# Attention a from a transposed copy of x with its norm behind the projection, the last norm's scale behind its linear layer, and a new order

## The chip, the cores and the metric

The kernel runs on one core of a Trainium2 chip. The metric is the time of one execution on the device in microseconds. Its engines are TensorE (PE, matrix products), VectorE (DVE), ScalarE (ACT), GpSimd (POOL) and SyncE (SP, which issues the DMAs). SBUF is the working memory, PSUM holds what TensorE writes: eight banks of 128 x 512 fp32.

## What is computed

Four blocks in a row on `x` of 4 batches x 256 rows x 512 columns, each behind a LayerNorm and with a residual:

```
x = x + attn_a(layernorm(x), Wqkv, bqkv, Wo, bo)     # one head, d = 128, softmax over 256 keys
x = x + ffn(layernorm(x), qweight, scale, zero, bias)
x = x + attn_b(layernorm(x), wq, wk, wv, wo)         # 32 heads of 16, rotary, causal
x = x + ffn(layernorm(x), qweight, scale, zero, bias)
return x

def layernorm(x):  return (x - mean(x)) / sqrt(var(x) + 1e-5)
def attn_a(x):     qkv = x @ Wqkv + bqkv;  q, k, v = split(qkv, 3)
                   return (softmax(q @ k.T / sqrt(128)) @ v) @ Wo + bo
def ffn(x):        weight = (unpack4(qweight) - zero) * scale     # [512 out, 512 in]
                   return x @ weight.T + bias
```

## The kernel before, in words

The work is cut into steps: a name, a batch `b` or a unit `u`, and a tile `t` of 128 rows (two tiles a batch). One list, PLAN, holds all 1004 steps. Each engine walks through the list and takes its own steps in that order, so the order in the list is the order on every engine; between engines there are semaphores, one for each kind of step. SP has its loads (D), stores and the copies between DRAM and SBUF in the same list, and issues them in order.

The steps around the change, in the kernel before:

- D loads: `x` by tile of 128 x 512, `wqkv` in two parts (columns of v, and of q and k), `bqkv`, `bias_o`, `q` (the packed weights), `ww` (the four weights of attention b, 1 MB each), and others.
- LN (DVE, L740 and L741) takes mean and variance. RS (GpSimd, L531 to L535) makes `rstd` and `offset` = -mean x rstd in four small instructions. NO (ScalarE, L602) writes the normed tile XN = x * rstd + offset. T (PE, L883) transposes it in four pieces, TH (ScalarE, L580) copies the transposed tile to `XT_hi` in the rounded type fp32r, and TL (DVE, L745) writes the rest, `XT_lo`. This chain stands in front of all four blocks; s = 1 to 4 in a step's name is the block.
- A product of two such pairs is three matmuls (`three_pass`, L859 to L861): low x high, high x low, high x high. QH, VH, QL and VL split Wqkv in the same way.
- Attention a of a batch: QV and QK project (q, k and v come out transposed), VC and QC copy them out with the bias, VA and AC transpose v back, SA is q k', AM the row maximum, AE the exponential, ET and EC its transpose, OA the product with v, OC its copy, WA the product with Wo (L931), WD (DVE, L768) divides by the sum and adds to X. BA (GpSimd, L541) adds the bias to X.
- ffn: F (PE, L941 and L942) is two matmuls for each piece of 128 inputs, FS (DVE, L774) adds the share of `zero`, FD (DVE, L782 and L784) multiplies by `scale` and adds to X. In the last block of batch 3 F and FD go by halves of 256 columns.
- Attention b: PJ, RO, RP, P1 to P3 project and rotate q and k; S, MX, ST, EX, MK, PV are the scores, the maxima, the exponentials, the mask and the product with v; NA, NX, NB, DH, DL carry the result to WO (PE), and OD (DVE, L788) adds it to X. OS stores.
- KP (PE, L869) are matmuls on `ident_h` whose results nobody reads.

Of the kernel before, what the change touches and what calls it, by code (L numbers as in the profile page):

```python
# [1062 lines left out]
```

## Time and profile before

| | |
|---|---|
| median of 3 runs | 273.88 us (273.66 to 274.55) |
| the profiled execution | 273.11 us, span of its trace 271.4 us |
| PE busy | 257.7 us, 95% |
| DVE busy | 225.8 us, 83% |
| GpSimd busy | 185.3 us, 68% |
| ScalarE busy | 145.2 us, 54% |
| DMA | 31.86 MB, mean 117 GB/s |

An engine's busy time is the union of its instructions' spans. The spans of matmuls overlap, since the next one enters while the one before drains; what one costs in a full stream is the distance from start to start. The span begins at 0 us with the first instruction; the execution's own time is 1.7 us longer. The clock that was granted to TensorE is shown as full in all 40 slices of the page.

### The profile page before, as it was taken

The numbers are of one execution on the slowest core, as the hardware profiler recorded it, in microseconds if no ns is written. First come the engines' busy times: TensorE is split into PE (matmuls) and PEld (weight loads), VectorE is DVE, ScalarE is ACT, GpSimd is POOL, SyncE is SP. The second block draws the span as 40 slices with busy tenths as digits, with TensorE's granted clock in tenths as the row PEclk, the third lists the DMA queues.
The fourth block names the chain that finished last, engine by engine and source line by source line (L and its number), as shares of the span: only waits on it lengthen the run. The fifth ranks groups of instructions, "written<-read, shape, count | busy, mean of one in ns | idle before, by whom it ended". The sixth has DMA issues, their size and how long they took to land.

```text
span 271.4 us, 6548 instructions
## 1 busy us (share of the span) xinstructions
PE 257.7 (95%) x2368; PEld 212.5 (78%) x2368; DVE 225.8 (83%) x402; ACT 145.2 (54%) x239; POOL 185.3 (68%) x229
## 2 busy tenths in 40 slices
PE   7698999999999999999999999999998999999984
PEld 2597878798989988778887988889677877785753
DVE  4575669668999998989868998998999988767886
ACT  2759796732774565365631767616634663277040
POOL 5887679989896889964568697287736663167070
PEclk9999999999999999999999999999999999999999
DMA  7999130202536237343343433343363333120112
GB/s 218 293 386 387 71 82 1 80 0 82 151 112 181 81 101 189 90 137 112 107 127 111 131 90 89 98 121 91 110 176 111 87 114 100 42 78 2 41 39 79
DMA packets 51192, 31.86 MB, mean 117 GB/s; under 512 B 5400, under 2 KB 46552, under 8 KB 51160
## 3 DMA queue, kind: packets, MB, share of 16 engines
q1 hardware_dynamic: 51160, 31.44, 38.5%
q8 instruction: 19, 0.31, 0.5%
q14 instruction: 13, 0.11, 0.1%
HBM read 22.91 MB, written 8.39 MB: 115 GB/s over the span
## 4 chain that ended last, share of the span: by engine, by line
PE 55%; POOL 13%; SPq 10%; DVE 6%; issue 6%; ACT 5%; DMA 3%; ACTq 0%; POOLq 0%; DVEq 0%
PE psum L859 10%; PE psum L860 9%; PE psum L861 9%; SPq L487 8%; PE psum L1026 7%; PE psum L1011 4%; PE psum L989 4%; POOL wb_lo L550 3%; POOL X L541 3%; POOL rstd L534 3%; PE psum L941 2%; PE psum L942 2%; PE psum L883 2%; PE psum L987 2%; PE psum L1013 2%
## 5 line engine op out<-in xcount | busy, mean ns | idle before, releaser
L573 POOL TENSOR_SCALAR_AFFINE_SELECT E<-E 128x512 f32<-128x512 f32 x64 | 41.5, 676 | 32.1 <-ACT E L699 32.0
L812 DVE TENSOR_REDUCE nmax<-psum 128x4 f32<-128x512 f32 (+1 forms) x64 | 59.2, 943 | 3.5 <-PE psum L989 3.5
L699 ACT ACTIVATE E<-psum 128x1536 f32<-128x1536 f32 x32 | 46.3, 1446 | 24.9 <-PE psum L1013 17.0
L859 PE MATMUL psum<-XT_lo,wb_hi 128*128 128x256 f32 x128 | 38.3, 299 | 0.3 <-POOL wb_lo L550 0.2
L860 PE MATMUL psum<-XT_hi,wb_lo 128*128 128x256 f32 x128 | 36.1, 282 | 0.0
L861 PE MATMUL psum<-XT_hi,wb_hi 128*128 128x256 f32 x128 | 36.1, 282 | 0.0
L602 ACT ACTIVATE XN<-X,offset,rstd 128x512 f32<-128x512 f32 x32 | 25.5, 810 | 19.2 <-POOL offset L535 19.2
L580 ACT ACTIVATE parts<-SH 128x512 bf16<-128x512 f32 x32 | 19.9, 626 | 25.4 <-POOL SH L562 17.2
L859 PE MATMUL psum<-wb_lo,XT_hi 128*128 128x256 f32 (+1 forms) x96 | 33.0, 344 | 0.0
L989 PE MATMUL psum<-QK 128*128 128x128 bf16 x256 | 30.2, 220 | 0.9 <-DMA QK<-qk_parts 0.6
L745 DVE TENSOR_TENSOR XT_lo<-psum,XT_hi 128x512 fp32r<-128x512 f32 x32 | 21.5, 682 | 11.0 <-ACT XT_hi L580 10.9
L860 PE MATMUL psum<-wb_hi,XT_lo 128*128 128x256 f32 (+1 forms) x96 | 30.6, 319 | 0.0
L861 PE MATMUL psum<-wb_hi,XT_hi 128*128 128x256 f32 (+1 forms) x96 | 30.5, 318 | 0.0
L1026 PE MATMUL psum<-E,V 128*32 128x128 f32 (+1 forms) x512 | 27.2, 331 | 1.6 <-POOL E L573 0.7
L941 PE MATMUL psum<-wf,XT_lo 128*128 128x512 f32 (+1 forms) x72 | 27.2, 387 | 0.1
L859 PEld LDWEIGHTS psum<-XT_lo,wb_hi 128*128 128x128 f32 x128 | 24.3, 190 | 2.6 <-DVE XT_lo L745 1.2
L942 PE MATMUL psum<-wf,XT_hi 128*128 128x512 f32 (+1 forms) x72 | 25.9, 369 | 0.0
L580 ACT ACTIVATE XT_hi<-psum 128x512 fp32r<-128x512 f32 x32 | 18.6, 598 | 13.1 <-PE psum L883 13.0
L740 DVE BATCH_NORM_STATS2 stats<-X 128x6 f32<-128x512 f32 x32 | 21.9, 684 | 4.4 <-DMA X<-L_attn_a_x 3.9
L1011 PE MATMUL psum<-QK 98*128 98x256 bf16 x128 | 24.8, 274 | 0.6 <-ACT E L699 0.4
L566 POOL TENSOR_TENSOR SH<-SH,parts 128x512 f32<-128x512 f32 x16 | 19.6, 1223 | 7.7 <-ACT parts L580 7.7
L860 PEld LDWEIGHTS psum<-XT_hi,wb_lo 128*128 128x128 f32 x128 | 24.4, 191 | 0.1
(97 smaller groups left out, 683.5 us busy)
## 6 DMA issues: line engine op xcount, KB each, us to landing
QK<-qk_parts SPq DMA_DIRECT2D x192, 64.0 KB
qk_parts<-parts SPq DMA_DIRECT2D x16, 384.0 KB, 2.9
X<-L_attn_a_x SPq DMA_DIRECT2D x8, 256.0 KB, 5.6
out<-X SPq DMA_DIRECT2D x6, 256.0 KB, 2.1
wb_raw<-L_attn_b_wq SPq DMA_DIRECT2D x1, 1024.0 KB, 9.7
wb_raw<-L_attn_b_wk SPq DMA_DIRECT2D x1, 1024.0 KB, 12.7
wb_raw<-L_attn_b_wv SPq DMA_DIRECT2D x1, 1024.0 KB, 15.0
wb_raw<-L_attn_b_wo SPq DMA_DIRECT2D x1, 1024.0 KB, 13.8
```

What stands on the lines that cost most here:

```text
L573: last = nc.gpsimd.affine_select(out=e, in_=e, compare_op=ALU.is_ge, fill=0.0, base=0, pattern=[[0, GH], [1, P]], channel_multiplier=-1)
L580: return nc.scalar.activation(out_, in_, ACT.Copy)
L699: nc.scalar.activation(E[:, n % 2], bank(3, 3), ACT.Exp, scale=float(HD) ** -0.5).then_inc(done[k], 1)
L812: nc.vector.tensor_reduce(nmax[:, u % 2, g::NG, t], (bank(1, 2) if t else bank(0)).rearrange("p (h k) -> p h k", h=GH), AX, ALU.max, negat ...
L859: nc.tensor.matmul(out_, stat[0], mov[1], start=first, stop=False)
L860: nc.tensor.matmul(out_, stat[1], mov[0], start=False, stop=False)
L861: return nc.tensor.matmul(out_, stat[0], mov[0], start=False, stop=last)
L941: nc.tensor.matmul(ps, XT_lo[:, slot, kt, tok], wf[:, kt, cols], start=kt == 0, stop=False)
L942: last = nc.tensor.matmul(ps, XT_hi[:, slot, kt, tok], wf[:, kt, cols], start=False, stop=kt == KT - 1)
L989: last = nc.tensor.matmul(ps[:, (j + 1) * width - P:(j + 1) * width], q[:, h, t * P:width], kk[:, h, t * P:width], start=True, stop=True)
L1011: nc.tensor.matmul(bank(3, 2)[:, j * S:(j + 1) * S], kk[0:SROWS, h, 0:P], q[0:SROWS, h, :], start=True, stop=True)
L1026: last = nc.tensor.matmul(ps[j * 32:(j + 1) * 32, kt * P:S], values(u // 2)[:, kt, (u % 2) * UH + NG * j + g], E[:, n % 2, at:at + S - kt ...
```

## The change

Attention a no longer needs the chain through T in front of it. The kernel gets a second input, `x_transposed`, x transposed by batch, 2 MB in all, made on the host beside the other inputs. XH (ScalarE) and XL (DVE) split it as it is, without the norm. QA projects x itself: the stationary side is a piece of `x_transposed`, the moving side 384 columns of Wqkv, so q, k and v come out by rows. The norm is applied afterwards: x_normed @ W = rstd * (x @ W) + offset * colsum(W). CS makes the column sums with a matrix of ones, CE copies them, Z (ScalarE) makes offset * colsum for a tile, QE (DVE) multiplies QA's sum by rstd and adds Z. QT transposes q and k; v is used as QE leaves it, so QV, QK, VC, VA and AC are gone. The bias of v goes through Wo once: BC spreads it, BM multiplies, BO adds it to `bias_o`. Wqkv is loaded and split in four pieces of 128 rows. Free buffers hold the raw pieces: XN, O and E for x, half of E for q, k and v, TR for the sums.

In the last block of batch 3 (SCALED_LATE), NO subtracts only the mean, and waits for LN instead of RS. RS makes `offset` = -rstd, RW multiplies the row sum by it, and FD multiplies the product by `offset` as well as `scale`.

PLAN is new as a whole, 1033 steps. KP at the start is 14 matmuls before and 8 now; at the end 2 x 5 before and 5 now.

```
-    ("D", "x", 0, 0), ("LN", 1, 0, 0), ("KP", 14), ("RS", 1, 0, 0), ("NO", 1, 0, 0), ("T", 1, 0, 0), ("D", "x", 0, 1),
+    ("D", "xt", 1, 0), ("D", "wqkv", 0), ("D", "xt", 0, 0), ("XH", 1, 0), ("XL", 1, 0), ("QH", 0), ("QL", 0), ("KP", 8),
...
+SCALED_LATE = (4, B - 1)
...
+        def tiles(b, i):
+            return slice(i, i + 1) if b == 0 else slice(2 * i, 2 * i + 2)
...
+        def raw(b, i):
+            if b < 2:
+                return XN[:, 2 * b:2 * b + 2].rearrange("p a (k n) -> p (a k) n", n=S)[:, tiles(b, i)]
+            if b == 2:
+                return O[:, tiles(b, i)]
+            return E[:, 0, 0:KT * S].rearrange("p (k n) -> p k n", n=S)[:, tiles(b, i)]
+
+        def qkv(b, t):
+            return E[:, 1, ((b % 2) * NT + t) * 3 * DA:((b % 2) * NT + t + 1) * 3 * DA]
...
+                    if (s, b) == SCALED_LATE:
+                        link(nc.gpsimd.tensor_scalar(mv[:, sl, ts, 1], mv[:, sl, ts, 1], EPS, None, ALU.add))
+                        link(nc.gpsimd.tensor_tensor(rstd[:, sl, ts], mv[:, sl, ts, 1], minus_half[:, ts], ALU.pow))
+                        nc.gpsimd.tensor_scalar(offset[:, sl, ts], rstd[:, sl, ts], -1.0, None, ALU.mult
+                                                ).then_inc(done[k], 1)
+                        continue
...
+                elif k == "XH":
+                    act.wait_ge(loaded["xt", *st[1:]], 16)
...
+                    copy(XT_hi[:, xt_of[st], tiles(*st[1:])], raw(*st[1:])).then_inc(done[k], 1)
...
+                    nc.scalar.activation(qkv(b, t), col_sum, ACT.Identity, scale=offset[:, b, t:t + 1]).then_inc(done[k], 1)
...
+                    if (s, b) == SCALED_LATE:
+                        act.wait_ge(done["LN"], upto("LN", s, b, t))
...
+                elif k == "XL":
...
+                    nc.vector.tensor_tensor(XT_lo[:, slot, part], raw(*st[1:]), XT_hi[:, slot, part].bitcast(F32),
+                                            ALU.subtract).then_inc(done[k], 1)
...
+                    nc.vector.scalar_tensor_tensor(qkv(b, t), bank(bank_of["QA", b, t, 0])[:, 0:3 * DA], rstd[:, b, t:t + 1],
+                                                   qkv(b, t), ALU.mult, ALU.add).then_inc(done[k], 1)
...
+                    for kt in range(KT):
+                        nc.tensor.matmul(ps, ones[:], wqkv_lo[:, kt], start=kt == 0, stop=False)
+                        last = nc.tensor.matmul(ps, ones[:], wqkv_hi[:, kt], start=False, stop=kt == KT - 1)
...
+                    for kt in range(KT)[tiles(b, i)]:
+                        last = three_pass(ps, [xt[:, slot, kt, t * P:(t + 1) * P] for xt in (XT_hi, XT_lo)],
+                                          [w[:, kt] for w in (wqkv_hi, wqkv_lo)], kt == 0, kt == KT - 1)
```

The loads at the start, as SP issues them. Before:

```order
L430 DMA X<-L_attn_a_x 128x512 x4
L432 DMA wqkv_raw<-L_attn_a_Wqkv 128x4x128
L432 DMA wqkv_raw<-L_attn_a_Wqkv 128x4x256
L437 DMA bias_o<-L_attn_a_bo 128x512
L430 DMA X<-L_attn_a_x 128x512 x2
L434 DMA bqkv_c<-L_attn_a_bqkv 128x3x1
```

Now (XN is the buffer that holds the raw pieces of `x_transposed` of batches 0 and 1, in pieces of 128 or 256 of the 512 inputs):

```order
L469 DMA XN<-x_transposed 128x512
L467 DMA wqkv_raw<-L_attn_a_Wqkv 128x384
L469 DMA XN<-x_transposed 128x256
L467 DMA wqkv_raw<-L_attn_a_Wqkv 128x384
L471 DMA bqkv_c<-L_attn_a_bqkv 128x3x1
L467 DMA wqkv_raw<-L_attn_a_Wqkv 128x384
L469 DMA XN<-x_transposed 128x256
L467 DMA wqkv_raw<-L_attn_a_Wqkv 128x384
L465 DMA X<-L_attn_a_x 128x512
```

The tiles of x themselves, which led the queue, now begin in ninth place; `bqkv` has moved from tenth to fifth.

The end on DVE, from the last low parts of attention b's output (`XT_lo<-O`) to the last blocks of batch 3. Before:

```order
L750 TENSOR_TENSOR XT_lo<-O,XT_hi 128x128
L745 TENSOR_TENSOR XT_lo<-psum,XT_hi 128x4x128
L750 TENSOR_TENSOR XT_lo<-O,XT_hi 128x128
L788 TENSOR_TENSOR X<-X,psum 128x512
L740 BN_STATS stats<-X 128x6
L741 BN_AGGR mv<-stats 128x2
L788 TENSOR_TENSOR X<-X,psum 128x512
L740 BN_STATS stats<-X 128x6
L741 BN_AGGR mv<-stats 128x2
L774 SCALAR_TENSOR_TENSOR X<-shift_r,row_sum,X 128x512
L782 TENSOR_TENSOR psum<-psum,scale_r 128x512
L784 TENSOR_TENSOR X<-X,psum 128x512
```

Now:

```order
L834 TENSOR_TENSOR XT_lo<-O,XT_hi 128x128 x2
L834 TENSOR_TENSOR XT_lo<-O,XT_hi 128x3x128
L829 TENSOR_TENSOR XT_lo<-psum,XT_hi 128x4x128
L879 TENSOR_TENSOR X<-X,psum 128x512
L824 BN_STATS stats<-X 128x6
L825 BN_AGGR mv<-stats 128x2
L860 SCALAR_TENSOR_TENSOR X<-shift_r,row_sum,X 128x512
L879 TENSOR_TENSOR X<-X,psum 128x512
L824 BN_STATS stats<-X 128x6
L825 BN_AGGR mv<-stats 128x2
L829 TENSOR_TENSOR XT_lo<-psum,XT_hi 128x4x128
```

OD (`X<-X,psum`) and LN of the second tile stood right behind those of the first; now FS of the batch before stands between them. On PE the four steps before the last ones were WO(3,1,0), WO(3,0,0), WO(3,1,1), WO(3,0,1); now they are WO(3,0,0), T(4,2,1), WO(3,0,1), WO(3,1,0), WO(3,1,1), and then T(4,3,0), F(4,2,1), F(4,3,0,0), five matmuls of KP, T(4,3,1) and the other three halves of F.

## Rows read from the trace of the kernel before

**Rows 1.** Head of the page: span, busy time and share by engine, instructions.
```profile
span 271.4 us, 6548 instructions
PE 257.7 (95%) x2368; PEld 212.5 (78%) x2368; DVE 225.8 (83%) x402; ACT 145.2 (54%) x239; POOL 185.3 (68%) x229
```

**Rows 2.** DVE by stretch: from:to, length, busy us (instructions), clock, DMA share, GB/s.
```profile
11.00:30.00 19.00, 12.74 (x24) 1.00 0.95 346
30.00:50.00 20.00, 14.41 (x28) 1.00 0.18 48
50.00:60.00 10.00, 6.63 (x14) 1.00 0.06 16
60.00:80.00 20.00, 18.27 (x32) 1.00 0.37 107
80.00:100.00 20.00, 19.90 (x34) 1.00 0.47 132
```

**Rows 3.** Timeline of the start: start, duration, engine, line, operation, tiles, shapes, count, idle before.
```profile
1.96 4.88 PE L869 MATMUL psum<-ident_h 128*128 128x512 bf16 x14 [1.96 <-POOL ident_h L518]
3.44 0.69 DVE L740 BATCH_NORM_STATS2 stats<-X 128x6 f32<-128x512 f32 x1 [3.44 <-DMA X<-L_attn_a_x]
4.93 0.15 PEld L869 LDWEIGHTS psum<-ident_h 128*128 128x128 bf16 x1 [0.28 <-issue]
5.35 0.99 PEld L869 LDWEIGHTS psum<-ident_h 128*128 128x128 bf16 x5 [0.27 <-issue]
11.04 0.36 PE L859 MATMUL psum<-XT_lo,wqkv_hi 128*128 128x256 f32 x1
```

**Rows 4.** Pieces of the chain of waits near 26 and 54 us: start, duration, what.
```profile
26.40 0.86 PE psum L931 x2
...
54.71 0.12 PE psum L861
54.83 0.22 PE psum L883 x2
```

**Rows 5.** Timeline of the last 20 us, columns as in rows 3.
```profile
251.34 0.50 PE L859 MATMUL psum<-wb_lo,XT_hi 128*128 128x512 f32 x1
252.78 0.71 DVE L825 STREAM_TRANSPOSE TR<-psum 128x512 f32<-128x512 f32 x1
256.82 0.39 PE L861 MATMUL psum<-wb_hi,XT_hi 128*128 128x512 f32 x1
257.05 0.39 PE L941 MATMUL psum<-wf,XT_lo 128*128 128x512 f32 x1
258.17 0.24 POOL L531 TENSOR_SCALAR mv<-mv 128x1 f32<-128x1 f32 x1 [7.67 <-DVE mv L741]
259.68 0.81 ACT L602 ACTIVATE XN<-X,offset,rstd 128x512 f32<-128x512 f32 x1 [4.41 <-POOL offset L535]
261.52 2.63 POOL L541 TENSOR_TENSOR X<-X,bias_f 128x512 f32<-128x512 f32 x2
262.83 1.87 DVE L774 SCALAR_TENSOR_TENSOR X<-shift_r,row_sum,X 128x512 f32<-128x512 f32 x1 [0.18 <-POOL X L541]
268.86 0.42 DVE L784 TENSOR_TENSOR X<-X,psum 128x256 f32<-128x256 f32 x1
```

**Rows 6.** Instructions by line and shape (busy us, mean ns, idle before), and L774 alone.
```profile
L883 PE MATMUL psum<-ident,XN 128*128 128x128 f32 x128 | 19.1, 277 | 3.5 <-ACT XN L602 3.4
L745 DVE TENSOR_TENSOR XT_lo<-psum,XT_hi 128x512 fp32r<-128x512 f32 x32 | 21.5, 682 | 11.0 <-ACT XT_hi L580 10.9
L750 DVE TENSOR_TENSOR XT_lo<-O,XT_hi 128x384 fp32r<-128x384 f32 x8 | 4.2, 551 | 1.0 <-ACT XT_hi L580 1.0
L774 DVE SCALAR_TENSOR_TENSOR X<-shift_r,row_sum,X x16: 697/742/1894, 35.8 to 266.1; 128x512 f32<-128x512 f32 x16
```

**Rows 7.** DMA of the first 30 us: GB/s in 40 slices of 0.75 us.
```profile
GB/s 0 0 57 358 358 287 248 326 317 354 302 212 191 334 196 256 392 403 410 399 380 385 391 393 388 382 352 363 401 374 385 390 396 388 382 385 374 224 71 38
```

**Rows 8.** PE from 11 to 25 us, columns as in rows 2.
```profile
11.00:25.00 14.00, 13.27 (x113) 1.00 1.03 377
```

More of the change, by code:

```diff
@@ L249, in bank_turns @@
             continue
-        if k not in READ_BY or (k in PAIRS and st[2]) or (k == "WO" and st[3]):
+        if k not in READ_BY or (k in PAIRS and st[2]) or (k in ("WO", "QA") and st[3]):
             continue
@@ L262, in xt_turns @@
     for st in PLAN:
-        if st[0] not in ("T", "DH"):
+        if st[0] not in ("T", "DH", "XH"):
+            continue
+        if st[0] == "XH":
+            b = st[1]
+            slot_of[st] = b % 2
+            if ("XH", b) not in readers:
+                readers["XH", b] = [r for t in range(NT) for r in readers.get((b % 2, t), [])]
+            before[st] = readers["XH", b]
+            for t in range(NT):
+                readers[b % 2, t] = [st for st in PLAN if st[:2] == ("QA", b)]
             continue
@@ L274, in xt_turns, with hybrid_block_kernel @@
     return slot_of, before
-def hybrid_block_kernel(nc, x, Wqkv, bqkv, Wo, bo, wq, wk, wv, wo, qweight, scale, zero, bias, rope, mask, out):
+def hybrid_block_kernel(nc, x, x_t, Wqkv, bqkv, Wo, bo, wq, wk, wv, wo, qweight, scale, zero, bias, rope, mask, out):
     nth, count = {}, {}
@@ L431, in _ @@
                     elif what == "wqkv":
-                        sp.dma_start(wqkv_raw[:, :, part_of[st[2]]], rows(Wqkv)[:, :, part_of[st[2]]]).then_inc(here, 16)
+                        sp.dma_start(wqkv_raw[:, st[2]], rows(Wqkv)[:, st[2]]).then_inc(here, 16)
+                    elif what == "xt":
+                        sp.dma_start(raw(st[2], st[3]), x_t[st[2]][:, tiles(st[2], st[3])]).then_inc(here, 16)
                     elif what == "bqkv":
@@ L884, in _ @@
                     last.then_inc(done[k], 1)
-                elif k in ("QK", "QV"):
+                elif k == "CS":
+                    pe.wait_ge(ones_ready, 1)
+                    pe.wait_ge(done["QL"], KT)
+                    ps = take(st)[:, 0:3 * DA]
+                    for kt in range(KT):
+                        nc.tensor.matmul(ps, ones[:], wqkv_lo[:, kt], start=kt == 0, stop=False)
+                        last = nc.tensor.matmul(ps, ones[:], wqkv_hi[:, kt], start=False, stop=kt == KT - 1)
+                    last.then_inc(done[k], 1)
+                elif k == "BM":
+                    pe.wait_ge(loaded["wo1",], 16)
+                    pe.wait_ge(done["BC"], 1)
+                    nc.tensor.matmul(take(st), bias_v, wo1[:], start=True, stop=True).then_inc(done[k], 1)
+                elif k == "QA":
+                    b, t, i = st[1:]
+                    slot = xt_of["XH", b, i]
+                    pe.wait_ge(done["XL"], upto("XL", b, i))
+                    if b < 2:
+                        pe.wait_ge(done["QL"], last_of(*[("QL", kt) for kt in range(KT)[tiles(b, i)]]))
+                    ps = (bank(bank_of["QA", b, t, 0]) if i else take(st))[:, 0:3 * DA]
+                    for kt in range(KT)[tiles(b, i)]:
+                        last = three_pass(ps, [xt[:, slot, kt, t * P:(t + 1) * P] for xt in (XT_hi, XT_lo)],
+                                          [w[:, kt] for w in (wqkv_hi, wqkv_lo)], kt == 0, kt == KT - 1)
+                    last.then_inc(done[k], 1)
+                elif k == "QT":
@@ L904, in _ @@
                                                 qkT[:, b % 2, 1], start=True, stop=True)
-                    last.then_inc(done[k], 1)
-                elif k == "VA":
-                    pe.wait_ge(done["VC"], upto("VC", st[1]))
-                    ps = take(st)
-                    for t in range(NT):
-                        last = nc.tensor.transpose(ps[:, t * DA:(t + 1) * DA], vT[:, t * P:(t + 1) * P], ident[:])
                     last.then_inc(done[k], 1)
@@ L1046, with laid_out @@
         "L0_ffn_bias"]
+def laid_out(inputs):
+    arrays = {n: np.ascontiguousarray(inputs[n]) for n in _INS}
+    x = arrays.pop("L0_attn_a_x")
+    x_t = x.transpose(0, 2, 1).reshape(B, KT, P, S).transpose(0, 2, 1, 3)
+    return {"L0_attn_a_x": x, "x_transposed": np.ascontiguousarray(x_t), **arrays,
+            "rope_table": rope_tables(), "mask_rows": mask_rows()}
 def kernel(**inputs):
```

161 lines of the change are left out of this document (98 added, 63 removed), and 266 rows, old and new, of the table PLAN.

## The prediction

> **What bounds the kernel now.** I read the head of the profile page first, then the engines' own rows for the start, then the last 20 us, then VectorE by stretch. The reader should see TensorE (PE) busy for 257.7 of 271.4 us and VectorE (DVE) for 225.8 [rows 1]. So the time is PE's work, plus what PE waits at the start and at the end, plus a middle in which DVE leaves little room: DVE is busy for 18.27 of 20 us in 60 to 80 and for 19.90 of 20 us in 80 to 100, but only for 12.74 of 19 and 14.41 of 20 between 11 and 50 [rows 2].
>
> At the start PE's busy time is mostly filler: 14 matmuls on `ident_h` from 1.96 us. The first matmul with data of Wqkv starts at 11.04 us [rows 3]. A matmul of 256 columns holds the stream for 0.12 us, two transposes of 128 columns for 0.22, the two halves of an fp32 product of 512 columns for 0.86 [rows 4]; one of 512 columns in fp32r takes 0.23 us (256.82 to 257.05, [rows 5]). These step widths, not the 280 ns durations (which overlap), are what I add up.
>
> **The change, part by part.** The profiled execution took 273.11 us, 0.77 below the median of 273.88; I sum against the first and put 0.77 on top.
>
> *PE work.* 32 calls of T (128 transposes, [rows 6]) become 24: out 8 x 4 x 0.11 = 3.5 us. VA's 8 transposes go: 0.9. Out go the 144 matmuls of 256 columns of QK and QV: 144 x 0.12 = 17.3. In come 96 of 384 columns in QA. No row has 384 columns; between 0.12 (256) and 0.23 (512) I take the middle, 0.175, so 16.8 (bounds 11.5 and 22.1, but the columns in all are equal, 36,864, so I keep the middle). In come also QT, 16 x 0.11 = 1.8; CS, 8 x 0.175 = 1.4; BM, 0.86. Sum: 20.9 in, 21.7 out, **-0.8 us**. The filler at the start shrinks from 14 to 8. Its weights enter every 0.42 us up to 5.35 us, then five in 0.99 [rows 3]: 512 columns in 0.42 us are the lower clock of 1.2 GHz, in 0.2 the upper of 2.4, although the page shows a full clock. Eight at 0.42 end where the clock rises, so I take 0; should it not have risen or fall back in the gap before QA, the first four calls go at half speed, +2.6 at most.
>
> *Start.* Before, the chain is x, LN, RS on GpSimd, NO, T, TH, TL, then QV. Up to 11.04 us PE does 3 calls of T, 1.3 us of useful work, and loses 9.7. In the new kernel QA needs only a load, XH and XL, and QH and QL. The first x tile lands for DVE at 3.44 us, when 0.26 MB had moved by about 2.9 us, so a landing lags the bytes by 0.5 us; the rate is then 250 to 360 GB/s [rows 7]. The new first loads are x_t(1,0) 0.26 MB, wqkv(0) 0.20, x_t(0,0) 0.13: landed at about 3.4, 4.3 and 4.5. ScalarE then makes XH(1,0), QH(0), XH(0,0) and DVE XL(1,0), QL(0), XL(0,0), each 0.3 to 0.7 us (0.682 for 512 columns on DVE, 0.551 for 384, [rows 6]): first QA at 5.9 us. Four calls run from there (2.6 us of work), but CS needs all four QL: 1.3 MB moved, plus `bqkv`, whose 384 pieces of 4 bytes now stand fifth in the queue and before the weights; I place wqkv(3) at 8.3, QL(3) at 9.4, CS to 10.8, BM (wo1 at 10.6) to 11.7. x_t(0,2) is thirteenth, 2.36 MB, landed at 10.9 and split at 11.7; the last five QA of batch 0 run to 14.3. By 14.3 us PE has done 7.5 us of useful work (8 x 0.525 for batch 0, 1.05, 1.4, 0.86) and lost 6.8 against 9.7: **-2.9 us**. Bounds: -5.1 if the loads never hold it (11.04 less 5.9), and 0 if the 2.1 MB of x_t, 5.4 us at 385 GB/s, delay the weights by as much as the start wins.
>
> *After the start* attention a of batch 0 is one long chain: QE, QT, QC, SA, AM, AE, ET, EC, OA. QE(0,0) ends at 15.1 and QC at about 16.6; SA stands behind QA(1,1,1) and ends at 17.8, AM at 18.7, the two halves of AE at about 20.1. PE has run out of QA for batches 0 and 1 at 18.8: a wait of 1.3 us, and another 0.4 us around OA(0). Before, PE is busy for 13.27 of the 14 us from 11 to 25, 0.7 us idle [rows 8]. **+1.0 us**, bounds -0.5 and +3.
>
> *DVE.* In: XL 10 (6 of 512 columns, 4 of 256, about 5.6 us), QE 8 of 384 columns with 0.551 to 0.682 each (4.9), QL 4 x 0.55 (2.2), BO (0.7). Out: TL 8 x 0.682 (5.5), the old QL (1.3). That is +6.6 us on an engine with about 15 us free between 11 and 60 [rows 2], while the start moves 3 us earlier and takes as much of that freedom away. It hides there in the main. What it costs if it doesn't is the second rival; I book **+0.8 us** for PE waits on QE and XL, bounds 0 and 7. ScalarE loses eight NO and two VC/AC chains, GpSimd loses VL; neither is the bound, so nothing for these.
>
> *End.* Today the last WO ends at 257.05 and the last X is ready at 269.28, 12.2 us later; stores take the other 2.1. Between them lies LN, then RS on GpSimd from 258.17, and ScalarE waits for RS until 259.68 [rows 5]. SCALED_LATE lets NO wait for LN alone, which takes 1.5 us out of the chain of each last tile; RS, RW and BA run beside T and TH, and FD takes the factor (one instruction in both forms). The new order also puts WO(3,1,*), 2.8 us, between the two tiles, so T(4,3,0) follows it without a wait, and F(4,2,1) (1.85) and F(4,3,0,0) (0.95) cover the second tile's LN and NO. From the last WO I work out: TL(4,3,0) at 2.4 us, FS, FD(4,2,1) to 4.5, FD(4,3,0,0) to 5.3, TL(4,3,1) to 6.5, F(4,3,1,*) to 8.5, three FD to 9.8. That is 2.4 us less. Against it, WO(3,0,1) now waits for NA(15) to DL(3,0,1), about 3.15 us after PV(15,1); PE has only WO(3,0,0) and T(4,2,1), 2.5 us, for it: +0.6 and small waits of 0.2. Today DVE starts NA(15) at 252.78, 1.4 us after PV(15,1), while PE works. **-1.6 us**, bounds -3 and +0.5.
>
> Sum: -0.8 - 2.9 + 1.0 + 0.8 - 1.6 = -3.5, so 269.6 for a profiled execution, **270.4 us** as a median.
>
> One row speaks against an edit: FS (L774), which reads two SBUF tiles, takes 742 ns in the median, but 1.87 us at 262.83 and up to 1.89, the one at 262.83 beside GpSimd adds [rows 5, 6]. XL reads two SBUF tiles where TL read one from PSUM. The Trainium skill says the same as a rule ("Advanced Engine Details and Errata", GPSIMD Details: GpSimd shares a read and a write interface with the DVE and conflicts with DVE instructions that have two SBUF inputs); by it every XL beside a GpSimd operation would be at risk, by the rows only some of FS are. The four XL of batches 2 and 3 stand where GpSimd has BA and WL: 4 x 1.15 = 4.6 us of DVE at worst, which the DVE term's upper bound of 7 holds.
>
> **Rivals.** *Only the end wins.* The loads eat the start: x_t adds 2.1 MB to a queue that is full until 28 us [rows 7], and RS, BA and WL on GpSimd, not PE, set when PJ can begin. For it: the chain of the first 50 us runs through GpSimd in several places. Against: the weights of WL are loaded at about 20 to 23 us, well ahead of use. Without the start term: 270.4 + 2.9 = 273.3; with part of it 272.
>
> *DVE takes over, and the kernel gets slower.* Place: 50 to 105 us, before the first NA. DVE has 6.6 us more to do there or before, has 3.6 us free between 60 and 100 at two bad stages [rows 2], and the new order puts more DVE work (about 9 us by my count of steps) ahead of the first MX. If the 6.6 and 4.6 us of stretched XL do not fit in the head, DVE falls behind by 6 to 8 us and PE waits for MX and NA: 270.4 - 0.8 + 7 = 276.6. It decides once PE's waits for DVE pass 4.3 us. For: 95% busy from 60 to 100. Against: a third of 11 to 60 is free, exactly where the additions stand.
>
> *The middle gets better.* The order is new everywhere, and ScalarE and GpSimd have a little less to do. If PE's short waits of the middle shrink by 3 us: 267.4. For: the two engines that feed DVE and PE get freer. Against: PE is full there already.
>
> **Numbers.** Forecast with its neighbourhood (268 to 272) 0.55, only the end wins (272 to 273.9) 0.14, slower through DVE 0.19, better middle 0.12. A difference under 0.3% (0.8 us) can't be told from none. Faster: 0.55 + 0.12 + most of 0.14, less a little, 0.76; same 0.06; slower 0.18. The range takes in half of each outer case: 266.0 to 276.0; the forecast's own is 268 to 272.
>
> **What would show it.** Right: the first 384-column matmul before 6.5 us, the last QA of batch 0 ending near 14.3 us; the next one after SA(0) waits about 1 us for AE; the step of QA near 0.175 us; PE busy 2 to 4 us less; the last WO about 10 us before the last X; NO released by DVE, not GpSimd, for the last two tiles. Wrong: first QA later than 8 us or a wait for DMA of more than 2 us after it (the first rival); DVE over 95% busy from 30 to 60, PE idle released by XT_lo, E or nmax with more than 4 us in total (the second); XL beside GpSimd at over 1 us; a wait before WO(3,0,1) of over 1.5 us.

## The result

The changed kernel takes 276.89 us (median of 22 runs, 273.92 to 279.1), the kernel before in the same sessions 274.12 (22 runs, 273.06 to 276.05). The ratio is 1.0063, 95% interval [1.0043, 1.0084]: slower by 0.4 to 0.8%, where 270.4 us and a range to 276.0 were forecast. The ratio leaves out the slow runs, those more than 1.5% above the fastest of their kernel (six of the changed kernel's 22); the medians of all runs are 2.77 us apart, 1.0%, and it is these 2.8 us that I account for below. The profiled execution took 276.74 us, its span is 275.0.

The head of the page of the changed kernel, against [rows 1]:

```profile
span 275.0 us, 6466 instructions
PE 253.9 (92%) x2295; PEld 210.0 (76%) x2295; DVE 230.1 (84%) x416; ACT 143.7 (52%) x237; POOL 185.8 (68%) x226
```

TensorE is busy for 3.8 us less and the span is 3.6 us longer, so TensorE stands idle for 7.4 us more. Where? I count "lost time": the time up to t, less the work that TensorE has begun by then, each matmul at its pace in a full stream (0.12 us for 256 columns, [rows 4]; 0.173 for 384), the filler as nothing. Up to 11, 25, 50, 85, 100, 150, 250 us and the end, the kernel before has lost 9.8, 10.8, 11.1, 12.5, 13.5, 17.2, 25.8 and 34.0 us, the changed one 7.2, 11.5, 14.4, 18.2, 18.7, 25.0, 31.1 and 38.4. The count depends on the paces taken, so read each figure to about 0.6 us. So the start is 2.6 us better at 11 us; that is gone by 25; between 25 and 85 the changed kernel loses 6.7 us, the other 1.7; between 100 and 150 it loses 2.6 us more and between 150 and 250 it gets 2.5 of them back, which no experiment here takes apart; and the end is better again.

The idle time alone, which needs no paces, says the same of the middle. TensorE's busy time from 25 to 100 us, before:

```profile
25.00:100.00 75.00, 74.36 (x553) 1.00 0.33 96
```

Now:

```profile
25.00:100.00 75.00, 70.35 (x485) 1.00 0.40 119
```

It stands idle for 0.6 us there before and for 4.6 now.

The start of the changed kernel in the timeline, against [rows 3]:

```profile
4.14 0.63 ACT L630 ACTIVATE XT_hi<-XN 128x512 fp32r<-128x512 f32 x1 [2.08 <-DMA XN<-x_transposed]
...
6.50 0.45 PE L954 MATMUL psum<-wqkv_lo,XT_hi 128*128 128x384 f32 x1 [1.22 <-DVE XT_lo L796]
...
7.64 0.34 PE L954 MATMUL psum<-wqkv_lo,XT_hi 128*128 128x384 f32 x1
...
8.16 0.34 PE L954 MATMUL psum<-wqkv_lo,XT_hi 128*128 128x384 f32 x1
...
11.74 0.24 POOL L574 TENSOR_SCALAR mv<-mv 128x2 f32<-128x2 f32 x1 [8.53 <-DVE mv L825]
...
13.47 1.13 PE L991 MATMUL psum<-wo,TR 128*128 128x512 f32 x2 [2.08 <-DMA wo<-L_attn_a_Wo]
...
22.89 0.66 PE L1025 MATMUL psum<-ident,EA 128*128 128x128 f32 x4 [0.79 <-ACT EA L714]
```

The first QA runs at 6.50 instead of 5.9; three matmuls of 384 columns take 0.52 us (7.64 to 8.16), 0.173 each, as forecast. Then BM waits 2.08 us for Wo, and GpSimd (POOL) begins its first RS only at 11.74 us.

All matmuls of T (L883 before, L978 now) between 30 and 90 us, and what their engine waited for (us, times; PE and its weight loads together, so a wait counts about twice). Before:

```profile
L883 PE MATMUL psum<-ident,XN x52: 270/273/329, 33.5 to 88.3; 128*128 128x128 f32 x52
...
  ACT XN L602: 0.6, 2
```

Now:

```profile
L978 PE MATMUL psum<-ident,XN x40: 271/273/332, 35.9 to 85.4; 128*128 128x128 f32 x40
...
  ACT XN L679: 10.8, 11
```

Fewer transposes, and they wait 10.8 us instead of 0.6. From the start of one matmul to the next, less its pace, PE itself waits 5.1 us at five places (the views count a matmul as busy while it drains, and so show 4.3): 0.83 at T(2,0,1) (35 us), 0.86 at T(3,0,1) (49), 0.54 and 0.81 at T(2,1,1) and T(2,2,1) (60 and 67), and 2.06 at T(3,1,0). The last of them, with what stands ahead of it on GpSimd and VectorE:

```profile
78.29 1.17 POOL L616 TENSOR_TENSOR SH<-SH,parts 128x512 f32<-128x512 f32 x1
...
79.42 1.30 POOL L596 TENSOR_TENSOR X<-X,bias_f 128x512 f32<-128x512 f32 x1
79.84 0.18 DVE L825 BATCH_NORM_AGGREGATE mv<-stats 128x2 f32<-128x6 f32 x1
...
80.81 0.55 POOL L574 TENSOR_SCALAR mv<-mv 128x2 f32<-128x2 f32 x1
...
81.44 0.58 POOL L576 TENSOR_SCALAR mv<-mv 128x2 f32<-128x2 f32 x1
...
82.09 1.07 POOL L577 TENSOR_TENSOR rstd<-mv,minus_half 128x2 f32<-128x2 f32 x1
...
83.24 0.19 POOL L578 TENSOR_TENSOR offset<-mv,rstd 128x2 f32<-128x2 f32 x1
83.47 1.52 ACT L679 ACTIVATE XN<-X,offset,rstd 128x512 f32<-128x512 f32 x2 [2.54 <-POOL offset L578]
...
84.34 0.66 PE L978 MATMUL psum<-ident,XN 128*128 128x128 f32 x4 [1.90 <-ACT XN L679]
```

The statistics are there at 80.02, four instructions on two columns take GpSimd from 80.81 to 83.43, then NO, then T. The same four took 1.63 us at 11.74 us; here, with VectorE at work on tiles in SBUF beside them (L896 at 80.16 us, FS at 81.19), they take 2.62. The engines by stretch (PE, PEld, DVE, ACT, POOL busy), against [rows 2]:

```profile
60.00:80.00 20.00, 18.98 (x129) 16.52 (x129) 17.73 (x35) 9.65 (x21) 19.11 (x22) 1.00 0.41 112
80.00:100.00 20.00, 18.10 (x166) 16.73 (x165) 17.64 (x29) 8.63 (x17) 16.53 (x15) 1.00 0.44 120
```

VectorE is less full than before (17.73 and 17.64 against 18.27 and 19.90); GpSimd is nearly full from 60 to 80 us (19.11; 18.05 before). And the end, against [rows 5]:

```profile
262.39 0.73 ACT L679 ACTIVATE XN<-X,mv 128x512 f32<-128x512 f32 x1 [2.30 <-DVE mv L825]
262.44 0.65 POOL L569 TENSOR_SCALAR mv<-mv 128x1 f32<-128x1 f32 x1 [5.60 <-DVE mv L825]
...
272.43 0.42 DVE L875 TENSOR_TENSOR X<-X,psum 128x256 f32<-128x256 f32 x1
```

NO(4,3,0) starts on VectorE's word, beside RS. The last WO matmul enters at 262.81 and X is ready at 272.85, 9.8 us after that matmul has passed; before, it was 12.2.

The runs of the changed kernel fall into two kinds by TensorE's mean clock: 10 of 22 at 0.998 or more, median 275.2, and 12 at 0.992 to 0.994, median 278.3. The profiled one was of the first kind, so its trace doesn't show the second. Of 116 runs of the kernel before for which the clock is on record, 92 were at 0.996 or more (median 273.9) and 24 below (274.2), so there it costs little.

### The profile page after: what moved, and what is told of

The parts are those of the page before. It is cut to its first block, busy times and chain, and to the rows that moved or that the text cites. A ratio compares the mean times of both kernels' runs of the same rounds, so it can differ in the third digit from the quotient of the medians.

```text
span 275.0 us, 6466 instructions
## 1 busy us (share of the span) xinstructions
PE 253.9 (92%) x2295; PEld 210.0 (76%) x2295; DVE 230.1 (84%) x416; ACT 143.7 (52%) x237; POOL 185.8 (68%) x226
## 4 chain that ended last, share of the span: by engine, by line
PE 41%; POOL 23%; SPq 13%; issue 7%; DMA 6%; DVE 6%; ACT 2%; POOLq 0%; ACTq 0%; DVEq 0%
SPq L522 11%; PE psum L954 7%; PE psum L955 6%; PE psum L956 6%; POOL X L596 6%; POOL wb_lo L601 5%; PE psum L1133 5%; POOL rstd L577 4%; PE psum L1096 4%; PE psum L1118 3%; PE psum L1048 3%; DMA QK<-qk_parts 2%; PE psum L1049 2%; PE psum L978 2%; DMA qk_parts<-parts 2%
## 5 line engine op out<-in xcount | busy, mean ns | idle before, releaser
L954 PE MATMUL psum<-wb_lo,XT_hi 128*128 128x256 f32 (+1 forms) x96 | 32.4, 337 | 0.6 <-DVE XT_lo L834 0.6
L1096 PE MATMUL psum<-QK 128*128 128x128 bf16 x256 | 28.8, 220 | 2.2 <-DMA QK<-qk_parts 2.2
L1133 PE MATMUL psum<-E,V 128*32 128x128 f32 (+1 forms) x512 | 25.4, 330 | 0.0
L679 ACT ACTIVATE XN<-X,offset,rstd 128x512 f32<-128x512 f32 x22 | 17.5, 807 | 14.8 <-POOL offset L578 14.8
L956 PEld LDWEIGHTS psum<-XT_hi,wb_hi 128*128 128x128 f32 x128 | 24.4, 191 | 0.0
L1096 PEld LDWEIGHTS psum<-QK 128*128 128x128 bf16 x256 | 20.7, 98 | 4.8 <-DMA QK<-qk_parts 2.9
L611 POOL TENSOR_TENSOR SH<-SH,table 128x512 f32<-128x512 f32 x16 | 21.5, 1346 | 3.4 <-DVE CC L890 3.4
L829 DVE TENSOR_TENSOR XT_lo<-psum,XT_hi 128x512 fp32r<-128x512 f32 x24 | 16.0, 678 | 8.7 <-ACT XT_hi L630 8.6
```

The source lines that it names most:

```text
L954: nc.tensor.matmul(out_, stat[0], mov[1], start=first, stop=False)
L956: return nc.tensor.matmul(out_, stat[0], mov[0], start=False, stop=last)
L1096: last = nc.tensor.matmul(ps[:, (j + 1) * width - P:(j + 1) * width], q[:, h, t * P:width], kk[:, h, t * P:width], start=True, stop=True)
L1133: last = nc.tensor.matmul(ps[j * 32:(j + 1) * 32, kt * P:S], values(u // 2)[:, kt, (u % 2) * UH + NG * j + g], E[:, n % 2, at:at + S - kt ...
```

## The experiments

Each kernel ran beside the kernel before; "full" is a run with a mean clock of 0.996 or more.

**1. The loads of the start.**

```
 e1: D(wo1), D(bias_o) behind D(x,1,1); BM behind QA(1,1,0); BO behind XL(1,1); BA(1,0,*) behind RS(1,1)
```

> The changed kernel with the loads of Wo and bias_o behind x(1,1) instead of ahead of x_t(0,2) and x(1,0); BM, BO and the first two BA stand later for it. Theory S (the start's win was lost to the queue of loads: TensorE waits 2.1 us for Wo at 13.5 us and x_t(0,2) lands at 13.8 us instead of 10.9): x_t(0,2) lands before 12 us, the last QA of batch 0 ends near 14 us instead of 16.9, and the time falls by 2 to 3 us, to about 274.5 us. Rival G (what comes after sets the pace: GpSimd's BA and WL and the chain of attention a in the first 50 us): the QA of batch 0 end earlier too, but PJ(0,0) stays within 0.5 us of its 54.3 us and the time within 1 us of the changed kernel's 276.9.

277.37 us (275.53 to 278.79), ratio 1.0125 [1.0089, 1.0162]. TensorE has lost 8.8 instead of 9.2 us at 14 us, and 13.8 instead of 14.4 at 50: the wait for Wo is gone, and the time is no better. So the loads of Wo and of the bias don't decide (the place of the x tiles in the queue stayed as it was). Its profile caught the low clock. TensorE by stretch: busy, clock, DMA share, GB/s:

```profile
80.00:84.40 4.40, 2.49 (x29) 1.00 0.52 150
84.40:87.80 3.40, 3.40 (x11) 0.50 0.31 85
```

TensorE is idle for 2 us at T(3,1,0), and then it works 3.4 us at the half level (1.2 GHz).

**2. The old order behind the new head.**

```
 e2: the new PLAN up to PJ(0,0), then the old one
```

> The changed kernel up to PJ(0,0), and from there all steps in the order that the kernel before has (with its ten filler matmuls at the end; RW behind RS). Theory O (TensorE loses 2.7 us more than before between 60 and 250 us because of the new order, for instance 1.5 us at 125 us for a load of QK): the lost time after PJ(0,0) is that of before, the kernel gets 2 to 4 us faster than the changed one, about 273.5 us. Rival D (the head leaves VectorE behind by several microseconds, and whatever order follows pays for it): no better than the changed kernel, 276 to 279 us, with more idle time of TensorE between 55 and 105 us.

283.0 us, 1.0335 [1.0302, 1.0368]. Worse, and mainly at one place: TensorE comes to T(2,1,1), in its old place in the order, at about 54.8 us, and its XN isn't there.

```profile
58.20 0.81 ACT L682 ACTIVATE XN<-X,offset,rstd 128x512 f32<-128x512 f32 x1 [5.46 <-POOL offset L581]
...
59.15 1.11 PE L981 MATMUL psum<-ident,XN 128*128 128x128 f32 x4 [4.29 <-ACT XN L682]
```

Behind this wait of 4.3 us the clock is at the half level for 6.8 us. So going back to the old middle doesn't help: the new order has T(2,1,1) at 61.1 us instead of 52.3, and the statistics come later there (LN of that batch ends at 56.12 us in this run). The order up to PJ(0,0) was not varied.

**3. Without the late scale at the end.**

```
-SCALED_LATE = (4, B - 1)
+SCALED_LATE = None          (and no RW steps)
```

> The changed kernel without SCALED_LATE: the last block of batch 3 normalizes as all others do, NO waits for RS again, RW is gone; the order is the same. Theory T (1.5 us of RS leaves the chain of each last tile, and most of it is on the path to the end): slower by 1 to 2 us than the changed kernel, 278 us or more. Rival (the new order covers RS anyway, since WO(3,1,*) and F(4,2,1) stand between): within 0.5 us of the changed kernel, 276.9 us.

279.65 us (276.74 to 282.05), 1.0182 [1.0141, 1.0222]; the two full runs 276.74 and 277.76 against 275.2. Two runs are few, but the late scale is worth some 2 us, as forecast.

**4. More filler at the start.**

```
-("KP", 8)
+("KP", 14)
```

> The changed kernel with 14 instead of 8 filler matmuls at the start, which keep TensorE busy until about 6.5 us. In 11 of 22 executions of the changed kernel the mean granted clock is 0.992 to 0.994, in the others 0.998 to 1.000, and the former are slower by 2 to 3 us. Theory K (the gap of 1.2 us behind eight fillers sometimes leaves the clock at its lower level for a few microseconds more): all runs at 0.998 or more, median near 275.2 us, 1.5 us faster than the changed kernel. Rival (the lower clock comes from a later gap, such as the one of 2.1 us ahead of BM): half of the runs still at 0.992 to 0.994, median near 276.9 us.

275.33 us (274.45 to 278.35, 11 runs), 1.0069 [1.0042, 1.0095]. 7 runs are full (median 274.96), 4 are at 0.994, and the profile, one of these, has the half level again right behind the wait at 82 us. So the start isn't where the clock falls. More runs were full (7 of 11 against 10 of 22), too few to tell from chance.

**5. Other work in the idle stretch.**

```
 e5: T(3,1,0), T(3,1,1) behind S(0,1,0) and ahead of F(2,2,1) -> behind F(2,2,1)
```

> The changed kernel with one edit on TensorE: the two transposes T(3,1,0) and T(3,1,1), for whose input TensorE stood idle 2.06 us at 82.2 us, stand behind S(0,1,0) and F(2,2,1), which has its input long before; the PSUM banks stay as they were. Theory W (the wait is a loss of its own): F(2,2,1), eight matmuls of 0.23 us, fills the gap, TensorE loses 1.9 us less by 85 us and keeps it; the dip to half clock behind the gap goes too: 274.6 to 275.3 instead of 276.9, hardly a run below full clock. Theory B (TensorE only waits there for GpSimd, which is late with everything behind it as well): the 1.9 us come back as waits before 110 us, the time stays at 276 to 277.

275.47 us, 1.0043 [1.0021, 1.0064]; 11 of 12 runs full, with a median of 275.4. That is the 275.2 of the changed kernel's own full runs: at 85 us TensorE had lost 1.9 us less, at 90 us only 0.8 and at 100 us 0.5. Theory B holds for the wait, and theory W for the clock.

**6. Filler in the idle stretch.**

```
+                    for _ in range(8 if st[1:] == (3, 1, 0) else 0):
+                        nc.tensor.matmul(ps..., ident_h[:], ident_h[:]..., start=True, stop=True)
                     pe.wait_ge(done["NO"], upto(*no))
```

> The changed kernel with eight filler matmuls (128x512, 0.21 us each, results never read) on TensorE ahead of T(3,1,0), in the 2.06 us in which it waits for XN there. They take no time that it had for anything else, so the gap stays and only the idleness goes. Theory C (the clock falls for 3.4 us in about half of the runs because TensorE stood idle in that gap, worth 2 to 3 us in those runs): nearly all runs at full clock, median at that of the changed kernel's full-clock runs, 275.0 to 275.6. Rival D (the low runs have another cause): about half of the runs still low, median 276.5 to 277.3.

275.0 us (273.94 to 276.38), 1.0027 [1.0008, 1.0046], all 12 runs full.

```profile
81.15 1.89 PE L980 MATMUL psum<-ident_h 128*128 128x512 bf16 x8
...
83.14 0.66 PE L985 MATMUL psum<-ident,XN 128*128 128x128 f32 x4
```

The transposes come no earlier for it; only the idleness went. (83.14 against the 84.34 above is the start of this one run: at 14.3 us it had lost 1.6 us less, and 1.2 at 80, before any filler.) So 1.9 of the 2.8 us are the clock, lost in about half of the runs behind one idle stretch.

**7. Less work on GpSimd.**

```
+                    w = 2 if s == 1 else BANK
-                    nc.gpsimd.tensor_tensor(X[:, b, t], X[:, b, t], (bias_o if s == 1 else bias_f)[:], ALU.add)
+                    nc.gpsimd.tensor_tensor(X[:, b, t, 0:w], X[:, b, t, 0:w], (... )[:, 0:w], ALU.add)
```

> The changed kernel with the eight additions of attention a's output bias to x on GpSimd (BA(1,b,t)) cut to 2 of 512 columns: that part of the computation is left out, about 1.1 us less of GpSimd's time at each, 8.8 us in all, between 15 and 60 us. Theory G (GpSimd sets the pace from about 15 to 86 us, and the change starts it later with the same work): the time lost on TensorE by 50 us falls from 13.8 to under 12, by 85 us from 18.2 to under 15, and the time to 272.5 to 274. Rival O (the places of the steps in the new order set it, whatever GpSimd does): under 1 us at 85 us, 276 to 277. The kernel before gets the same edit in the run beside it.

> The kernel before with the same edit (the eight additions of attention a's output bias on GpSimd cut to 2 of 512 columns, that part left out). GpSimd stands idle 3.4 and 1.9 us in the first two tens of microseconds there and 3.1 and 2.5 in the next two, so it has some slack: theory G expects less than in the changed kernel, 272.8 to 273.6 against 273.9. Rival O: no change within 0.5 us in either. If both kernels gain the same, GpSimd is a bound of both but not what the change made worse.

274.1 us (full runs 273.4), 0.9973 [0.9950, 0.9997], and for the kernel before 273.04, 0.9967 [0.9944, 0.9991]. In full runs the changed kernel gains 1.8 us, the other 1.3 (272.7 against 274.0). GpSimd's load counts in both, by the full runs hardly more now, and of the 5.7 us between them at 85 us it explains a small part: at 85 us the changed kernel had lost about 16 us, where theory G wanted under 15, and the wait at T(3,1,0) stayed at 2.05 us.

**8. No wait for the statistics.**

```
-                    act.wait_ge(done["RS"], ...)
+                    act.wait_ge(done["LN"], upto("LN", s, b, t))        (for s in 2, 3)
+                    by = {"bias": offset[:, b, t:t + 1], "scale": rstd[:, b, t:t + 1] if s == 2 else 0.05}
```

> The changed kernel in which the two middle norms (before the linear layer and before attention b) don't wait for their statistics on GpSimd: NO(2,*) scales with the statistics of the first norm and NO(3,*) with 0.05, so the result is another one; GpSimd still works out the statistics (three short instructions for a batch instead of four), only LN on VectorE is waited for. Theory N (the extra loss between 25 and 85 us is TensorE waiting at its transposes T for the path LN, GpSimd's RS of 1.6 to 3 us behind what stands in its queue, NO): the gaps at 34, 48, 60, 66 and 82 us go, the time lost by 85 us falls from 17.1 to 18.2 to 14 or less, the time to 272 to 273.5 and no run is below full clock. Rival B (those waits only mark that everything behind is late too; TensorE waits later instead): under 1 us at 100 us, 274.5 to 275.5. The kernel before gets the same edit beside it.

> The kernel before with the same edit (NO(2,*) scales with the first norm's statistics, NO(3,*) with 0.05, neither waits for RS on GpSimd; another result). Its trace has no wait at a transpose over 0.4 us between 25 and 100 us. Theory N: 273.2 to 274, nothing gained, so the difference between the two kernels closes or turns round. Rival B: the same small change as in the changed kernel.

271.72 us (270.94 to 273.21), 0.9927 [0.9902, 0.9953], all runs full. The edit also takes one of the four instructions out of each RS, in both kernels. The waits of T between 30 and 90 us in the changed kernel's variant:

```profile
  ACT XN L683: 0.9, 2
```

From 25 to 100 us:

```profile
25.00:100.00 75.00, 73.12 (x520) 1.00 0.42 125
```

TensorE is idle for 1.9 us, against 4.6 in the changed kernel and 0.6 in the kernel before. So 2.8 of the 4.0 us between the two kernels go with the wait. What stays is mostly one new wait, for VectorE's maxima:

```profile
80.05 0.40 PE L1100 MATMUL psum<-QK 128*128 128x128 bf16 x4 [1.34 <-DVE nmax L907]
```

The kernel before with the same edit takes 275.85 us, 1.0075 [1.0045, 1.0106]: slower, where 273.2 to 274 were expected. Its trace shows why. With RS shorter, GpSimd's BA and WL come beside FS on VectorE, which took 0.75 and 0.74 us in the kernel before:

```profile
36.31 1.76 DVE L788 SCALAR_TENSOR_TENSOR X<-shift_r,row_sum,X 128x512 f32<-128x512 f32 x1 [3.70 <-POOL X L550]
...
39.01 5.18 POOL L559 TENSOR_TENSOR wb_lo<-wb_raw,wb_hi 128x1024 fp32r<-128x1024 f32 x2 [1.48 <-ACT wb_hi L589]
39.20 2.75 DVE L788 SCALAR_TENSOR_TENSOR X<-shift_r,row_sum,X 128x512 f32<-128x512 f32 x1
...
42.60 0.50 PE L955 MATMUL psum<-wf,XT_lo 128*128 128x512 f32 x1 [1.74 <-DVE XT_lo L759]
```

TensorE waits 0.52 and 1.74 us for the XT_lo behind them. From 50 to 100 us, away from this place, it is idle for 0.1 us, against 0.5 without the edit: the kernel before had next to nothing to gain there. This is the pair that tells the theories apart: the path LN, RS on GpSimd, NO is what the change made critical. It doesn't tell how much of the path's lateness comes from a GpSimd that begins late, from RS slowed beside VectorE, or from the places in the new order.

**9. More loads in the kernel before.**

```
+ six D("more", n), 256 KB each, behind D(x,2,1), D(q), D(ww,0), D(x,3,0), D(zs)
```

> The kernel before with six further loads of 256 KB (1.5 MB, what the changed kernel loads of x_t for batches 1 to 3) issued between x(2,1) and the second matrix of attention b, into space that isn't in use there; nothing reads them. Theory D (the transposed copy costs time because all loads behind it land later, 1.5 MB at 383 GB/s is 3.9 us): 275.5 to 277.5. Rival H (what stands behind in the queue, the matrices of attention b, the scales and bias of the linear layer, has slack): 273.7 to 274.6, and the loads of the change are hidden.

273.65 us, 0.9981 [0.9956, 1.0006]. The rate from 20 to 40 us rises (321 and 55 GB/s before, now 382 and 144), the time doesn't. So 1.5 MB of extra loads, as many as `x_transposed` adds for batches 1 to 3, cost nothing as bytes behind the start.

**10. F(2,1) earlier.**

```
 e12: F(2,1,*) ahead of PJ(3,0); FS(2,1,0), FD(2,1,*), LN(3,1,*) behind WD(3,1); RS(3,1) behind BA(2,2,1)
 f3:  the same, and RS(2,3) behind RS(3,1)
```

> The changed kernel in another order at 65 to 83 us: F(2,1,0) and F(2,1,1) stand ahead of PJ(3,0) on TensorE, FS(2,1,0), FD, LN(3,1,*) behind WD(3,1) on VectorE, RS(3,1) behind BA(2,2,1) on GpSimd. XN for T(3,1,0) is then ready at about 79 us, and TensorE comes there at 82. Theory M (the chain from F(2,1) over FD, LN, RS and NO to T(3,1) and PJ(4,0) is what bounds there, and filling the gap with other work gave nothing in full-clock runs for that reason): the 2.06 us go and stay gone, 273.2 to 274.3 with no run below full clock. Rival V (VectorE, without an idle time over 0.3 us from 64 to 83 us, bounds there in any order): the wait turns up at another step, 274.8 to 275.6.

> As e12_f21_earlier, but with RS(2,3) behind RS(3,1) on GpSimd, as LN(2,3,*) stands behind LN(3,1,*) on VectorE; there GpSimd stood 6.8 us at RS(2,3) with everything queued behind it. Theory M (the chain F(2,1), FD, LN, RS, NO, T(3,1) bounds here): the wait at 82 us goes without another, 273.4 to 274.6, no run below full clock. Rival V (VectorE and GpSimd are full from 64 to 83 us, what is put first makes something else late): a wait of 1 us or more at another step, 275 to 277.

286.66 us, 1.0448 [1.0408, 1.0489], and 280.75, 1.0241 [1.0215, 1.0266]. In the first, LN(2,3,*) had moved back on VectorE, but RS(2,3) stood in its old place on GpSimd:

```profile
69.25 1.18 POOL L619 TENSOR_TENSOR SH<-SH,parts 128x512 f32<-128x512 f32 x1
...
77.19 0.57 POOL L577 TENSOR_SCALAR mv<-mv 128x2 f32<-128x2 f32 x1 [6.77 <-DVE mv L828]
```

One waiting instruction held the whole queue for 6.8 us, and by 95 us TensorE had lost 26.6 us, against 17.3 with the filler alone (experiment 6). The second mends that and still waits 1.6 us at T and 3.4 us at the next S, for nmax. Theory M fell. V held in kind (what is put first there makes something else late), but it had 275 to 277 and not 280.75.

**11. The late scale for norm 2 as well.**

```
-SCALED_LATE = (4, B - 1)
+SCALED_LATE = {(2, 0), (2, 1), (2, 2), (2, 3), (4, B - 1)}     (RW(2,b,t) ahead of BA(2,b,t))
```

> The changed kernel with the late scaling, which it has for the last norm, for the four norms ahead of the first linear layer too (norm 2 of batches 0 to 3): NO(2,*) only subtracts the mean, the scale comes with FD(2,*), RW(2,*) stands ahead of BA(2,*) on GpSimd; the result is the same. Theory N: the waits at T(2,0), T(2,1) and T(2,2), 0.83, 0.54 and 0.81 us at 35, 60 and 67 us, go; those at T(3,0) and T(3,1) stay, and with the latter the low clock in part of the runs: lost on TensorE by 80 us 1.5 to 2 us less, time 274.5 to 275.5. Rival B (given back: the chain to T(3,1) starts no earlier, since GpSimd and VectorE have as much to do): 276.5 to 277.2, the wait at 82 us grows instead.

> The kernel before with the late scaling for norm 2 of batches 0 to 3. Its trace has no such waits over 0.4 us but the one at 52.6 us. Theory N: no gain, 273.5 to 274.6. Rival (the late scaling is good for any of them): 272 to 273.

277.29 us, 1.0105 [1.0076, 1.0134], no run of 6 full; the kernel before with it 275.69, 1.0064 [1.0040, 1.0087], again slower than expected and with the same picture as in experiment 8 (two FS of 1.90 and 2.49 us beside GpSimd at 35.8 and 38.8 us). In the changed kernel TensorE has lost 11.9 us at 75 us, as the kernel before (11.9; the changed kernel 15.8), and then gives it all back at T(3,1,0). GpSimd's RS(3,1) and the clock there:

```profile
77.87 0.65 POOL L578 TENSOR_SCALAR mv<-mv 128x2 f32<-128x2 f32 x1
...
80.65 1.52 ACT L683 ACTIVATE XN<-X,offset,rstd 128x512 f32<-128x512 f32 x2 [2.99 <-POOL offset L582]
```

```profile
80.40:87.20 6.80, 5.69 (x21) 0.50 0.29 81
```

A wait of 3.4 us, and 6.8 us at the half level behind it. Theory N held for the waits before 75 us, its rival for the time.

**12. Both, and the same without the idle stretch.**

```
 f4: f1's late scale, f3's order, ("KP", 14) at the start
 g2: f1, and 14 filler matmuls ahead of T(3,1,0)
 g1: f1, and 8 filler matmuls; for RS(3,0), RS(3,1) the -1.0 and the EPS on VectorE (two tensor_scalar on 128x2)
```

> The changed kernel with f1's late scaling, f3's order and 14 instead of 8 filler matmuls at the start. Theories N and M add up: 271.7 to 273, below both kernels, no run below full clock. If the two work on one chain and VectorE or GpSimd bounds: no better than the better of the two, 273.5 to 275.

> f1_late_scale_mid with 14 filler matmuls (0.21 us each, results never read) ahead of T(3,1,0), in the 3.4 us that TensorE waits there. Theory C (the idle stretch costs the clock, nothing else makes f1 slower than e8_filler_in_gap): all runs at full clock, 274.6 to 275.4, as e8 with 275.0, since T(3,1,0) comes at the same 81.2 to 81.5 us in both. Rival: low clock and 276.5 to 277.5 as f1, if something else lowered the clock; or 273 to 274, if the waits taken away earlier are a gain of their own.

> f1_late_scale_mid with two further edits, the result the same: in RS(3,0) and RS(3,1) the sign of the mean and the addition of the epsilon, two of the four instructions (0.65 and 0.58 us and their distances, 1.4 us at RS(3,1)), are done on VectorE behind LN (two instructions on 128x2), and 8 filler matmuls stand ahead of T(3,1,0) in place of the idle time. Theory P (T(3,1) is bound by the chain LN, RS, NO on a full GpSimd, one for one): T(3,1,0) at 79.8 to 80.4 us instead of 81.5, lost by 100 us 16 to 16.5, 273.3 to 274.2 at full clock, 1.0 to 1.6 us less than g2_filled. Rival V (VectorE, with two instructions more, bounds): T(3,1,0) at 81 or later, the same as g2_filled.

f4: 278.99 us, 1.0185 [1.0150, 1.0219], f3's trouble again. g2: 273.21 us, 0.998 [0.9959, 1.0001], all 12 runs full. g1: 273.01 us (271.74 to 273.81), 0.9966 [0.9945, 0.9987], all full: it leaves nothing of the computation out and is 0.1 to 0.6% below the kernel before. (In the expectations I had put T(3,1,0) of the kernel with filler at 81.2 us; that is where its filler starts, the transposes run at 83.14.) In g1:

```profile
81.23 0.66 PE L996 MATMUL psum<-ident,XN 128*128 128x128 f32 x4 [0.83 <-ACT XN L687]
```

T(3,1,0) is at 81.23 us against 82.77 in g2, 1.5 us earlier. But 0.7 of them were there at the first T already (33.95 against 34.65), ahead of both edits of RS, and 0.9 at T(2,2,0) (71.63 against 72.49), so about 0.7 us belong to RS(3,1), for 1.3 us taken out of it: theory P's "one for one" isn't shown. The time shows only 0.2 us of it, too little to tell from none. g2 came out where its rival had it (273 to 274), 1.8 us below the kernel with filler alone: with the idleness filled, the three waits taken away at 35, 60 and 67 us do stay gone in part (from 25 to 100 us it loses 6.0 us, g1 5.5, against 7.4 with filler alone). Why not in whole is open.

## Why the prediction was wrong

*PE work, -0.8:* right. All matmuls at their pace make 237.4 us before and 236.6 now.

*Start, -2.9:* at 11 us it was -2.6, QA was 0.6 us later than forecast. But I let the term end at 14.3 us, and there 0.7 were left in the profiled run, 2.3 in the one of experiment 6: BM and the late x_t(0,2) take more or less of it by how the loads fall (the last QA of batch 0 ends near 16.9 us in the profiled run and not near 14.3).

*After the start, +1.0:* by 25 us the lost time is 0.7 us above before in the profiled run, and 0.6 below it (10.2) in experiment 6. I had -2.9 + 1.0 = -1.9. So here 1.3 to 2.6 us are missing.

*DVE, +0.8, and "GpSimd loses VL; neither is the bound, so nothing for these":* this is the step that failed. From 25 to 100 us the changed kernel loses 7.2 us, before 2.7, and by idle time alone 4.6 against 0.6; I had booked 0.8, on the wrong engine. I asked what GpSimd no longer does and not when it can begin. It starts on the statistics at 11.74 us, behind x tiles that stand ninth in the queue, and must bring the same RS, BA, WL and rotations by the same time. Before, its first RS began at 4.56 us. Both kernels begin the first WL at about 28.3 us; by then GpSimd had done six BA and the first RS of all four batches before, and has done four BA and three of those RS now. Between 20 and 86 us it is busy for 59.9 us against 54.8. Before:

```profile
20.00:86.00 66.00, 54.77 (x58) 1.00 0.36 114
```

Now:

```profile
20.00:86.00 66.00, 59.91 (x63) 1.00 0.45 143
```

With so little slack there, each RS (2.6 us for four instructions on two columns at 81 us) stands in front of a transpose, and experiment 8 shows the price: 3.3 us against the kernel with filler (275.0, all runs full), 5.2 against the median. That before is not faster without the wait, and has next to no such wait in its trace, speaks for its being the change's doing. That the late x tiles are what makes GpSimd late is argued from these counts; no run moved them forward. The Trainium skill ("Perfetto Trace Analysis", Optimizing GPSIMD Operations) advises to prefer other engines where possible; g1's T(3,1,0), about 0.7 us earlier, agrees, its time hardly.

*The clock:* I took 0, with the start as the only place of risk. It falls in the middle, in about half of the runs, for 1.9 us of the median (experiment 6).

*End, -1.6:* right, nearly to the number. From PV(15,1) to the end of the span it was 20.8 us (250.6 to 271.4) and is 19.1 (255.9 to 275.0): -1.7. From the last WO to the last X 9.8 us were forecast and measured; experiment 3 gives the late scale about 2 us.

*The row against the edit:* the Trainium skill ("Advanced Engine Details and Errata", GPSIMD Details) and FS's 1.87 us [rows 5, 6] let XL beside GpSimd seem at risk. No XL was stretched; the four that this row leaves out took at most 0.693 us, and the worst FS 1.15:

```profile
L796 DVE TENSOR_TENSOR XT_lo<-XN,XT_hi x6: 392/426/693, 4.8 to 18.1; 128x256 fp32r<-128x256 f32 x4, 128x512 fp32r<-128x512 f32 x2
```

But that hardly tests the row: only three of the ten XL ran beside a GpSimd instruction at all (at 18.12, 33.00 and 34.13 us), and there it was GpSimd's that grew, to 0.77, 1.23 and 0.54 us for steps of an RS that take 0.24, 0.72 and 0.19 alone. FS did grow in a variant, to 2.75 us (experiment 8), so such a conflict does show in the traces, and either side can lose by it.

*The rivals.* "DVE takes over" had 276.6, nearly the time measured, for a reason that isn't so; had it been the forecast, the number would have been luck. DVE is at 17.6 to 17.7 of 20 us from 60 to 100, and the waits are for NO on GpSimd's word. (It also misread its row: 18.27 and 19.90 of 20 us leave 1.8 us free, not 3.6.) It comes next, though: with the wait for NO gone, TensorE waits for VectorE's maxima (experiment 8). "Only the end wins" named GpSimd's RS, BA and WL and was closest to the mechanism, but it priced them at no more than the start's gain, and named the loads, which experiments 1 and 9 clear as far as they go (Wo, the bias, and bytes behind the start). "The middle gets better" had it the wrong way round.

The account of +2.8 us: work -0.8, clock +1.9, end -1.7, and the rest of the waits +3.4, of which the statistics' path carries 3.3 (experiment 8). The +3.4 is what is left over and not measured, and the 3.3 comes from other runs, so their agreement is no proof that nothing else is in it.
